# Projections of a fused attention and feed-forward block in another order: values, gates, latent query and key, then key and query

## The chip, the cores and the metric

The kernel runs on one core of a Trainium2 chip. The metric is the device time of one execution in microseconds (us). The kernel before was timed three times: 748.38, 748.62 and 749.38 us, median 748.62. One execution was also profiled. The core's engines run side by side, each through its own list of instructions in order: TensorE (PE for its matmuls and PEld for its weight loads), VectorE (DVE), ScalarE (ACT), GpSimd (POOL) and SyncE (SP, which issues most DMAs here). They wait for one another by semaphores.

## The reference, cut to what matters

The input x is 32 batches of 256 rows by 128 columns, all float32. Each batch goes through one adaptive-layernorm block:

```
h = layernorm(x) * (1 + ca) + sa                # scale and shift per batch, from a small matmul
Q, K, V = h @ wq, h @ wk, h @ wv                # 16 heads of 8
local = softmax(window-masked Q K^T / sqrt(8)) @ V    # window of 32, blocks of 32 against 64
GQ = h @ wgq                                    # 8 heads of 8, latent query
GK, GV = mean4(h @ wgk), mean4(h @ wgv)         # 64 latents: means over 4 rows
rem = softmax(causal GQ GK^T / sqrt(8)) @ GV @ r_out_w
out = (sigmoid(Q . gate_local) * local + sigmoid(Q . gate_remote) * rem) @ w_out
x = x + ga * out
x = x + gb * ffn(layernorm(x) * (1 + cb) + sb)  # per-batch mixed weights, 512 wide, gelu
```

## The kernel before

Everything stays on chip. The batches run through a software pipeline of 36 steps, `for it in range(4)`, a hardware loop over it = 4 to 31 (28 passes of the same instructions), and four more steps. In step `it` the kernel works on several batches at once: layernorm of batch it, projections and scores of batch it - 1, softmax output and gating of batch it - 2, output projection of batch it - 3, second layernorm and the gate of the feed-forward of batch it - 4. After the pipeline comes the feed-forward part, eight batches at a time, which the change does not touch.

There is no scheduler. Each engine has a function `step(it)` whose order is written by hand, and the order of the work is that of the five lists and the semaphores between them. PSUM is eight banks, SB0 to SB3 (scores and their transposes) and WB0 to WB3 (everything else); `bank_free` makes TensorE wait until the last reader of a bank is through.

What the steps around the change do, with the lines of the kernel before:

- TensorE, `projections(it)` (lines 831 to 856), the first thing in its step: key and query (wk, wq) into WB0, after VectorE has read the latent scores there (semaphore `ls_sub`); latent query and key (wgq, wgk) into WB1; values (wv) into WB3; two gates (gate_w) into WB2, after ScalarE has read the last batch's gates from there (`tg_ready`). Then `latent_T` (line 899): transposes of the latent probabilities into WB0 once ScalarE has copied the query out of it (`qt_ready`) and into WB1; `probs_T` (line 888): transposes of the probabilities Pr into SB0 to SB3; later `latent_values`, the transpose of xn_d (line 994), `values` with its row sums on PT_sum (lines 927 and 931), and at the end of the step `latent_scores` and `scores` of batch it - 1 (lines 970, 871 to 882).
- ScalarE, `step` (line 405): copies K_ch and QT (key and query) out of WB0, then exponentials Pr 1, GQT and GKT (latent query and key) out of WB1, Pr 2, V_rows (values) out of WB3, Pr 3, then the copies PL and PT of the transposed probabilities, xn_d and h2T (second layernorm), hT, and the exponentials PlA, PlB, the gates' tanh (tg) and Pr 0. The exponentials of batch it - 2 wait for VectorE (`s_sub`), one each.
- GpSimd, `step` (line 331): KM, four copies of the key each masked to some of the heads, from K_ch (line 336); then the small operations on the layernorm statistics, ve_a and rstd_a of batch it and ve_d, neg_d, rstd_d, shift_d of batch it - 4; then PT_sum in two halves (line 358), GKBD, the residual addition, attT.
- VectorE, `step` (line 595): statistics of both layernorms, xn_a, the latent and local normalisations (rlden; rden, line 634, and a_loc, which frees bank SB2 for the next scores), gating, then latent maxima, lowered latent scores (PlA, PlB), and maxima and lowered scores Pr 0 to Pr 3.
- SyncE: stores V_rows when copied and loads it again spread out (VBD).

Of the kernel before, what the change touches and what calls it, by code (L numbers as in the profile page):

```python
# [14 lines left out]
D = 128  # L15
# [9 lines left out]
def adaln_block(nc, ins, out):  # L25
# [17 lines left out]
    with ExitStack() as ctx:  # L43
# [143 lines left out]
        def at_least(eng, s, value):  # L187

            if not isinstance(value, int) or value > 0:
                eng.wait_ge(s, value)  # L190
# [203 lines left out]
        @block.scalar  # L394
        def _(act):
            act.wait_ge(mod_loaded, N_MOD)
            nc.scalar.activation(silu_a[:], c_rows[:], ACT.Exp, scale=-1.0).then_inc(silu_exp, 1)
            act.wait_ge(siluT_done, 1)
            nc.scalar.copy(siluT[:], WB[1][:, 0:B]).then_inc(siluT_ready, 1)

            def probs(b, k):
                act.wait_ge(s_sub, 4 * b + (k + 1))
                nc.scalar.activation(Pr[:, k, :], Pr[:, k, :], ACT.Exp).then_inc(p_ready, 1)  # L403

            def step(it):
                if has(it, 1):

                    b = it - 1
                    act.wait_ge(qk_done, b + 1)
                    at_least(act, km_ready, b)  # L410
                    nc.scalar.copy(K_ch[:], WB[0][:, S:2 * S]).then_inc(k_ready, 1)  # L411
                    nc.scalar.copy(QT[:], WB[0][:, 0:S]).then_inc(qt_ready, 1)
                if has(it, 2):
                    probs(it - 2, 1)
                if has(it, 1):
                    act.wait_ge(gqk_done, b + 1)
                    nc.scalar.activation(GQT[0:NL], WB[1][0:NL, 0:S], ACT.Copy, scale=SCALE / POOL).then_inc(gq_ready, 1)
                    nc.scalar.copy(GKT[:], WB[1][0:NL, S:S + NL]).then_inc(gq_ready, 1)
                if has(it, 2):
                    probs(it - 2, 2)  # L420
                if has(it, 1):

                    b = it - 1
                    act.wait_ge(v_done, b + 1)
                    at_least(act, vbd_loaded, N_VBD * b)
                    nc.scalar.copy(V_rows[:].rearrange("p t n -> p (t n)"), WB[3][:, 0:T * D]).then_inc(vrows_ready, 1)
                if has(it, 2):
                    probs(it - 2, 3)
                if has(it, 2):
                    b = it - 2  # L430
                    if isinstance(it, int) and it == 2:
                        act.wait_ge(ga_stored, 16)

                    act.wait_ge(lpt_done, 2 * b + 1)
                    nc.scalar.copy(PL[:, :, 0:S].rearrange("p g (t s) -> p t g s", t=T),  # L435
                                   WB[0][:].rearrange("p (t g s) -> p t g s", t=T, g=LG)).then_inc(lpt_copied, 1)
                    act.wait_ge(lpt_done, 2 * b + 2)
                    nc.scalar.copy(PL[:, :, S:S + P],
                                   WB[1][:, 0:2 * P].rearrange("p (g s) -> p g s", g=LG)).then_inc(lpt_copied, 1)
                    for q in range(4):  # L440

                        act.wait_ge(pt_done, 4 * b + (q + 1))
                        nc.scalar.copy(PT[:, q * 2 * S:(q + 1) * 2 * S], SB[q][:]).then_inc(pt_copied, 1)  # L443
                if has(it, 4):
                    b = it - 4
                    act.wait_ge(shift_ready, b + 1)
                    at_least(act, x2T_done, b)
                    for t in range(T):
                        nc.scalar.activation(xn_d[:, t, :], x_all[:, bass.ds(b * S + t * D, D)], ACT.Identity,  # L449
                                             scale=rstd_d[:, t:t + 1], bias=shift_d[:, t:t + 1]).then_inc(xn_d_s, 1)  # L450
                    act.wait_ge(x2T_done, b + 1)
                    nc.scalar.activation(h2T[:, bass.ds(b * S, S)], SB[0][:, 0:S], ACT.Identity,
                                         scale=cb1T[:, bass.ds(b, 1)], bias=sbT[:, bass.ds(b, 1)]).then_inc(h2T_ready, 1)
                    act.wait_ge(hid_done, b + 1)

                    nc.scalar.activation(SB[1][:, 0:S], SB[1][:, 0:S], ACT.Relu, bias=gate_b1[:],  # L456
                                         accum_out=hsum[:, bass.ds(b, 1)]).then_inc(hid_summed, 1)
                if has(it, 0):

                    act.wait_ge(xT_done, it + 1)  # L460
                    at_least(act, hp_ready, it)
                    if isinstance(it, int) and it == 0:
                        act.wait_ge(mod_ready, 4)
                    nc.scalar.activation(hT[:], SB[0][:, 0:S], ACT.Identity, scale=ca1T[:, bass.ds(it, 1)],
                                         bias=saT[:, bass.ds(it, 1)]).then_inc(hT_ready, 1)
                if has(it, 1):
                    b = it - 1
                    for t, pl in ((0, PlA), (1, PlB)):
                        act.wait_ge(ls_sub, 2 * b + (t + 1))
                        nc.scalar.activation(pl[:], pl[:], ACT.Exp).then_inc(pl_ready, 1)  # L470

                    act.wait_ge(gates_done, b + 1)
                    at_least(act, ag_ready, b)
                    at_least(act, remg_ready, b)
                    nc.scalar.activation(tg[:].rearrange("p k s -> p (k s)"), WB[2][:], ACT.Tanh, scale=0.5
                                         ).then_inc(tg_ready, 1)
                    probs(b, 0)

            def after(it):
                if it == 0:  # L480
                    act.wait_ge(wqT_done, 1)
                    nc.scalar.copy(wqT, SB[1][:, 0:D]).then_inc(wqT_ready, 1)
                    act.wait_ge(gate_w_done, 1)
                    for k in range(2):
                        nc.scalar.copy(gate_w[:, k, :].rearrange("p (h d) -> p h d", d=HD),
                                       bc(SB[2][:, k * H:(k + 1) * H], [P, H, HD], 2)).then_inc(gate_w_ready, 1)
                if it == 1:

                    act.wait_ge(wT_done, 1)
                    nc.scalar.copy(W1T[:], WB[3][:]).then_inc(wT_ready, 1)  # L490
                    act.wait_ge(wT_done, 2)
                    nc.scalar.copy(W2T[:].rearrange("p c h -> p (c h)"), WB[3][:]).then_inc(wT_ready, 1)
                    act.wait_ge(wT_done, 3)
                    nc.scalar.copy(gate_w1T[:], WB[3][:, 0:P]).then_inc(wT_ready, 1)
                    nc.scalar.copy(gate_w2T[:], WB[3][:, P:P + E]).then_inc(wT_ready, 1)

            pipeline(act, step, after)

            with act.Fori(0, NG) as g:
                for j in range(GB):  # L500

                    act.wait_ge(ffn1_done, g * GB + (j + 1))
                    if j >= 2:
                        act.wait_ge(ffn2_done, g * GB + (j - 1))
                    for c in range(FC):
                        nc.scalar.activation(u[j % 2][:, c, :], WB[2 * (j % 2) + c // 2][:, (c % 2) * S:(c % 2 + 1) * S],  # L506
                                             ACT.Gelu_apprx_tanh, bias=mb1T[:, c, bass.ds(g * GB + j, 1)]
                                             ).then_inc(gelu_done, 1)
# [266 lines left out]
        def _(pe):  # L775
# [55 lines left out]
            def projections(it):  # L831
                b = it - 1
                pe.wait_ge(hT_ready, b + 1)
                bank_free(pe, it, (2, ls_sub, 2, 2))
                mm(WB[0][:, S:2 * S], wk[:], hT[:], start=True, stop=True)  # L835
                mm(WB[0][:, 0:S], wq[:], hT[:], start=True, stop=True).then_inc(qk_done, 1)
                pe.wait_ge(hp_ready, b + 1)
                bank_free(pe, it, (2, ls_sub, 2, 1))
                mm(WB[1][0:NL, 0:S], wgq[:], hT[:], start=True, stop=True)
                mm(WB[1][0:NL, S:S + NL], wgk[:], hpT[:], start=True, stop=True).then_inc(gqk_done, 1)  # L840
                bank_free(pe, it, (3, remg_ready, 1, 1), (2, vrows_ready, 1, 1))
                if isinstance(it, int) and it == 1:
                    pe.wait_ge(attn_w_ready, 1)
# [10 lines left out]
                for k in range(2):  # L854
                    last = mm(WB[2][:, k * S:(k + 1) * S], gate_w[:, k, :], hT[:], start=True, stop=True)
                last.then_inc(gates_done, 1)

            def scores(it):

# [278 lines left out]
```

## Time and profile before

| | before |
|---|---|
| median of three runs | 748.62 us |
| the profiled execution | 748.97 us, its span 747.2 us |
| mean granted TensorE clock over the span | 0.979 of full speed |
| busy share: TensorE matmul, weight load | 86%, 68% |
| busy share: VectorE, ScalarE, GpSimd | 72%, 52%, 39% |
| chain that ended last, by engine | PE 42%, DVE 26%, ACT 15%, no visible wait 14% |
| pipeline steps | from about 8 us to 563 us; one pass of the loop 16.34 us |
| feed-forward part | about 563 us to the end |

The shares are averages over two parts with different limits. In the feed-forward part TensorE is nearly always busy; in the pipeline no engine is, and what sets its pace has to be read from one pass. Times are counted from the start of the span.

### The profile page before, as it was taken

To read this page: it belongs to the slowest core of one execution; us is meant where nothing else is said; L and a number is where in the kernel's file an instruction comes from. 1 tells how busy PE (TensorE), PEld (TensorE's weight loads), DVE (VectorE), ACT (ScalarE), POOL (GpSimd) and SP (SyncE) were. 2 spreads that over 40 slices of the span, in tenths; PEclk is the share of its full clock that TensorE was granted. 3 is DMA by queue.
4 is the path that set the end of the run, shared out by engine and by line. 5 is a ranking of instruction groups with operands and counts; after the bars stand their busy time and mean duration, and the time that the engine had idled before them with its cause. 6 is when DMAs were issued, how large, how long until landed. Compare 5 with 4: busy or idle time off the path is not lost.

```text
span 747.2 us, 24120 instructions
## 1 busy us (share of the span) xinstructions
PE 645.6 (86%) x8822; PEld 506.4 (68%) x8822; DVE 538.1 (72%) x1241; ACT 384.9 (52%) x910; POOL 294.9 (39%) x415
## 2 busy tenths in 40 slices
PE   5588888788888878888887888888779999999998
PEld 3366666566666656666665666666558999898996
DVE  5568788888878888887888888788755546273552
ACT  2256655666665566666555666655543223423233
POOL 2256555455555545555554555555530000000000
PEclk9699999999999999999999999999978999999999
DMA  3757111000101100010110001010140010100101
GB/s 99 174 78 96 32 24 32 21 21 21 28 22 24 31 21 21 21 28 21 24 32 21 21 21 28 21 24 18 29 44 0 10 35 15 32 24 21 34 9 49
DMA packets 65797, 24.84 MB, mean 33 GB/s; under 512 B 38440, under 2 KB 64360, under 8 KB 65648
## 3 DMA queue, kind: packets, MB, share of 16 engines
q1 hardware_dynamic: 64320, 18.25, 10.2%
q0 software_dynamic: 1456, 6.31, 5.6%
q8 instruction: 14, 0.23, 0.1%
q14 instruction: 7, 0.06, 0.0%
HBM read 16.13 MB, written 8.40 MB: 33 GB/s over the span
## 4 chain that ended last, share of the span: by engine, by line
PE 42%; DVE 26%; ACT 15%; issue 14%; POOL 1%; ACTq 1%; DVEq 1%; DMA 0%; SPq 0%; POOLq 0%
DVE mx L561 10%; PE SB L820 7%; PE WB L808 7%; DVE rden L634 5%; ACT PT L443 5%; PE SB L927 5%; PE WB L795 4%; PE SB L795 4%; ACT xn_d L449 4%; DVE Pr L568 3%; ACT Pr L403 3%; PE SB L882 2%; PE SB L931 2%; ACT PL L435 2%; PE WB L970 2%
## 5 line engine op out<-in xcount | busy, mean ns | idle before, releaser
L336 POOL TENSOR_TENSOR KM<-K_ch,bd_scale 128x1024 f32<-128x1024 f32 x32 | 60.6, 1893 | 125.2 <-ACT K_ch L411 125.2
L634 DVE RECIPROCAL rden<-SB 128x256 f32<-128x256 f32 x32 | 56.2, 1758 | 54.5 <-PE SB L931 54.5
L506 ACT ACTIVATE Pr<-WB,mb1T 128x256 f32<-128x256 f32 x128 | 49.8, 477 | 75.7 <-PE WB L808 75.6
L561 DVE TENSOR_REDUCE mx<-SB 128x8 f32<-128x512 f32 x128 | 87.2, 681 | 1.5 <-PE SB L882 1.5
L403 ACT ACTIVATE Pr<-Pr 128x512 f32<-128x512 f32 x128 | 80.8, 631 | 10.8 <-DVE Pr L568 7.2
L568 DVE TENSOR_TENSOR Pr<-SB,mx 128x512 f32<-128x512 f32 x128 | 84.6, 681 | 0.0
L358 POOL TENSOR_TENSOR PT_sum<-PT 128x512 f32<-128x512 f32 x64 | 80.3, 1275 | 3.8 <-ACT PT L443 3.8
L443 ACT COPY PT<-SB 128x512 f32<-128x512 f32 x128 | 66.1, 622 | 0.0
L896 PE MATMUL SB<-ident,Pr 128*128 128x128 f32 x512 | 63.0, 276 | 0.9 <-ACT Pr L403 0.9
L820 PE MATMUL SB<-Pr,GA 128*128 128x256 f32 x256 | 61.2, 381 | 0.0
L835 PE MATMUL WB<-hT,wk 128*128 128x256 f32 x64 | 23.3, 448 | 43.2 <-DVE PlB L582 43.2
L808 PE MATMUL WB<-h2T,mW 128*128 (+1 forms) x256 | 60.2, 380 | 0.0
L896 PEld LDWEIGHTS SB<-ident,Pr 128*128 128x128 f32 x512 | 57.8, 143 | 1.8 <-ACT Pr L403 1.8
L377 POOL TENSOR_TENSOR attT<-a_gated,rem_g 128x256 f32<-128x256 f32 x32 | 23.2, 725 | 88.8 <-DVE a_gated L647 85.7
L470 ACT ACTIVATE PlA<-PlA 128x256 f32<-128x256 f32 x32 | 13.3, 416 | 79.5 <-DVE PlA L582 79.5
L808 PEld LDWEIGHTS WB<-h2T,mW 128*128 128x128 f32 x256 | 48.2, 190 | 6.4
L820 PEld LDWEIGHTS SB<-Pr,GA 128*128 128x128 f32 x256 | 46.1, 190 | 6.2 <-DVE GA L675 1.2
L835 PEld LDWEIGHTS WB<-hT,wk 128*128 128x128 f32 x64 | 10.0, 196 | 57.7 <-DVE PlB L582 53.7
L882 PE MATMUL SB<-KM,QT 32*32 32x256 f32 x2048 | 48.4, 387 | 0.0
L970 PE MATMUL WB<-GKBD,GQT 128*128 128x512 f32 (+1 forms) x128 | 47.9, 498 | 0.0
L456 ACT ACTIVATE SB<-SB,gate_b 128x256 f32<-128x256 f32 x32 | 14.3, 448 | 63.8 <-PE SB L1011 63.8
L615 DVE RECIPROCAL rlden<-WB 128x128 f32<-128x128 f32 x32 | 30.7, 958 | 19.7 <-PE WB L946 19.7
(195 smaller groups left out, 1518.5 us busy)
## 6 DMA issues: line engine op xcount, KB each, us to landing
x_all<-in_L_attn_x SPq DMA_DIRECT2D x32, 128.0 KB, 2.1
v_rows<-V_rows SPq DMA_DIRECT2D x32, 128.0 KB, 1.8
VBD<-v_rows SPq DMA_DIRECT2D x128, 32.0 KB, 1.8
TW<-in_L_ffn_TW POOLq DMA_DIRECT2D x16, 256.0 KB, 9.5
GA<-ga_rows POOLq DMA_DIRECT2D x1, 2048.0 KB, 10.5
out_x<-attT SPq DMA_DIRECT2D x16, 128.0 KB, 1.8
out_x<-y_ga SPq DMA_DIRECT2D x16, 128.0 KB, 1.8
PT<-in_L_ffn_W SPq DMA_DIRECT2D x2, 256.0 KB
```

The source lines that it names most:

```text
L336: nc.gpsimd.tensor_tensor(KM[:, :, W:KW], bc(K_ch[:], [P, 4, S], 1), bc(bd_scale[:], [P, 4, S], 2), ALU.mult).then_inc(km_ready, 1)
L358: nc.gpsimd.tensor_tensor(PT_sum[:, pair, :], both[:, pair, 0, :], both[:, pair, 1, :], ALU.add).then_inc(pts_ready, 1)
L403: nc.scalar.activation(Pr[:, k, :], Pr[:, k, :], ACT.Exp).then_inc(p_ready, 1)
L443: nc.scalar.copy(PT[:, q * 2 * S:(q + 1) * 2 * S], SB[q][:]).then_inc(pt_copied, 1)
L561: nc.vector.tensor_reduce(mx[:, k, :], SB[k][:].rearrange("p (h j) -> p h j", h=8), AX.X, ALU.max).then_inc(mx_ready, 1)
L568: nc.vector.tensor_tensor(Pr[:, k, :].rearrange("p (w h c) -> p h w c", w=2, h=8), SB[k][:].rearrange("p (h w c) -> p h w c", w=2, h=8), b ...
L634: nc.vector.reciprocal(rden[:], SB[2][:, S:2 * S]).then_inc(rden_ready, 1)
L808: last = mm(WB[2 * (j % 2) + c // 2][:, (c % 2) * S:(c % 2 + 1) * S], mW1[:, j, c * P:(c + 1) * P], h2T[:, bass.ds((g * GB + j) * S, S)], ...
L820: last = mm(SB[j % 2][:, 0:S], mW2[:, c, j, :], u[j % 2][:, c, :], start=(c == 0), stop=(c == FC - 1))
L882: last = mm(SB[g][W * q:W * q + W, 4 * HALF * t:4 * HALF * (t + 1)].rearrange("p (h j) -> p h j", h=4), QT[rows, W * blk:W * blk + W], KM[ ...
L896: last = nc.tensor.transpose(SB[q][:, k * P:(k + 1) * P], Pr[:, q, o:o + P], ident[:])
L970: mm(WB[1 - t][:, 0:8 * m].rearrange("p (h j) -> p h j", h=8), GQT[:, t * P:(t + 1) * P], GKBD[:, :, 0:m], start=True, stop=True).then_inc ...
```

## The change

The order of the four projections on TensorE becomes values, gates, latent query and key, key and query; ScalarE's copy of the values moves to where key and query were copied, and the other way round. All instructions, banks, sizes and semaphores stay; every wait moves with its instruction.

```diff
@@ ScalarE, step
                 if has(it, 1):
 
                     b = it - 1
-                    act.wait_ge(qk_done, b + 1)
-                    at_least(act, km_ready, b)
-                    nc.scalar.copy(K_ch[:], WB[0][:, S:2 * S]).then_inc(k_ready, 1)
-                    nc.scalar.copy(QT[:], WB[0][:, 0:S]).then_inc(qt_ready, 1)
+                    act.wait_ge(v_done, b + 1)
+                    at_least(act, vbd_loaded, N_VBD * b)
+                    nc.scalar.copy(V_rows[:].rearrange("p t n -> p (t n)"), WB[3][:, 0:T * D]).then_inc(vrows_ready, 1)
                 if has(it, 2):
                     probs(it - 2, 1)
...
-                    act.wait_ge(v_done, b + 1)
-                    at_least(act, vbd_loaded, N_VBD * b)
-                    nc.scalar.copy(V_rows[:].rearrange("p t n -> p (t n)"), WB[3][:, 0:T * D]).then_inc(vrows_ready, 1)
+                    act.wait_ge(qk_done, b + 1)
+                    at_least(act, km_ready, b)
+                    nc.scalar.copy(K_ch[:], WB[0][:, S:2 * S]).then_inc(k_ready, 1)
+                    nc.scalar.copy(QT[:], WB[0][:, 0:S]).then_inc(qt_ready, 1)
                 if has(it, 2):
                     probs(it - 2, 3)
@@ TensorE, projections
                 pe.wait_ge(hT_ready, b + 1)
-                bank_free(pe, it, (2, ls_sub, 2, 2))
-                mm(WB[0][:, S:2 * S], wk[:], hT[:], start=True, stop=True)
-                mm(WB[0][:, 0:S], wq[:], hT[:], start=True, stop=True).then_inc(qk_done, 1)
-                pe.wait_ge(hp_ready, b + 1)
-                bank_free(pe, it, (2, ls_sub, 2, 1))
-                mm(WB[1][0:NL, 0:S], wgq[:], hT[:], start=True, stop=True)
-                mm(WB[1][0:NL, S:S + NL], wgk[:], hpT[:], start=True, stop=True).then_inc(gqk_done, 1)
                 bank_free(pe, it, (3, remg_ready, 1, 1), (2, vrows_ready, 1, 1))
...
                 last.then_inc(gates_done, 1)
+                pe.wait_ge(hp_ready, b + 1)
+                bank_free(pe, it, (2, ls_sub, 2, 1))
+                mm(WB[1][0:NL, 0:S], wgq[:], hT[:], start=True, stop=True)
+                mm(WB[1][0:NL, S:S + NL], wgk[:], hpT[:], start=True, stop=True).then_inc(gqk_done, 1)
+                bank_free(pe, it, (2, ls_sub, 2, 2))
+                mm(WB[0][:, S:2 * S], wk[:], hT[:], start=True, stop=True)
+                mm(WB[0][:, 0:S], wq[:], hT[:], start=True, stop=True).then_inc(qk_done, 1)
```

TensorE at the head of the hardware loop before; "x2" is two instructions of one form, and the lines that are not matmuls load or compute the value of a wait.

```order
L190 ISA
L835 MATMUL WB<-hT,wk 128x256
L836 MATMUL WB<-hT,wq 128x256
L190 REGISTER_ALU
L839 MATMUL WB<-hT,wgq 64x256
L840 MATMUL WB<-hpT,wgk 64x64
L847 MATMUL WB<-wv,hT 128x128 x2
L190 REGISTER_ALU
L855 MATMUL WB<-hT,gate_w 128x256 x2
L901 REGISTER_ALU
L904 MATMUL WB<-ident,PlA 128x128 x2
```

The same place in the changed kernel.

```order
L190 REGISTER_ALU
L840 MATMUL WB<-wv,hT 128x128 x2
L190 REGISTER_ALU
L848 MATMUL WB<-hT,gate_w 128x256 x2
L190 ISA
L852 MATMUL WB<-hT,wgq 64x256
L853 MATMUL WB<-hpT,wgk 64x64
L190 REGISTER_ALU
L855 MATMUL WB<-hT,wk 128x256
L856 MATMUL WB<-hT,wq 128x256
L904 MATMUL WB<-ident,PlA 128x128 x2
```

Key and query have moved from first to last, right ahead of the latent transposes (L904), which wait for the copy of the query.

ScalarE from the head of the loop before to its copy PL; Pr rows are the exponentials 1, 2 and 3.

```order
L411 COPY K_ch<-WB 128x256
L412 COPY QT<-WB 128x256
L402 ISA
L403 ACTIVATE Pr<-Pr 128x512
L417 ACTIVATE GQT<-WB 64x256
L418 COPY GKT<-WB 64x64
L402 REGISTER_ALU
L403 ACTIVATE Pr<-Pr 128x512
L190 REGISTER_ALU
L426 COPY V_rows<-WB 128x256
L402 REGISTER_ALU
L403 ACTIVATE Pr<-Pr 128x512
```

The same place in the changed kernel.

```order
L411 COPY V_rows<-WB 128x256
L402 ISA
L403 ACTIVATE Pr<-Pr 128x512
L416 ACTIVATE GQT<-WB 64x256
L417 COPY GKT<-WB 64x64
L402 REGISTER_ALU
L403 ACTIVATE Pr<-Pr 128x512
L425 COPY K_ch<-WB 128x256
L426 COPY QT<-WB 128x256
L402 REGISTER_ALU
L403 ACTIVATE Pr<-Pr 128x512
```

K_ch and QT now stand behind the exponential Pr 2; V_rows stands ahead of Pr 1. VectorE's, GpSimd's and SyncE's own lists are the same as before.

## Rows read from the trace of the kernel before

**Rows 1.** Timeline, VectorE, one loop pass: start, us, engine, line, operation, count, [idle before <-releaser]

```profile
306.49 1.76 DVE L634 RECIPROCAL rden<-SB 128x256 f32<-128x256 f32 x1 [1.75 <-PE SB L931]
...
322.83 1.76 DVE L634 RECIPROCAL rden<-SB 128x256 f32<-128x256 f32 x1 [1.75 <-PE SB L931]
```

**Rows 2.** Timeline, the same pass, from VectorE's last lowered scores to the row sums

```profile
315.12 1.28 DVE L568 TENSOR_TENSOR Pr<-SB,mx 128x512 f32<-128x512 f32 x2
...
315.83 0.63 ACT L403 ACTIVATE Pr<-Pr 128x512 f32<-128x512 f32 x1 [0.20 <-DVE Pr L568]
...
316.37 0.35 ACT L426 COPY V_rows<-WB 128x256 f32<-128x256 f32 x1
316.62 0.63 ACT L403 ACTIVATE Pr<-Pr 128x512 f32<-128x512 f32 x1
...
317.15 0.57 ACT L435 COPY PL<-WB 128x512 f32<-128x512 f32 x1
...
317.88 2.06 ACT L443 COPY PT<-SB 128x512 f32<-128x512 f32 x4
...
319.79 0.93 ACT L449 ACTIVATE xn_d<-x_all,shift_d,rstd_d 128x128 f32 x2
...
320.77 0.44 PE L994 MATMUL SB<-ident,xn_d 128*128 128x128 f32 x2 [0.89 <-ACT xn_d L449]
...
322.15 0.62 PE L931 MATMUL SB<-PT_sum,ones_bd 128*32 128x256 f32 x8
```

**Rows 3.** Timeline, the same pass, key and query copies and GpSimd's work behind them

```profile
313.98 0.35 ACT L411 COPY K_ch<-WB 128x256 f32<-128x256 f32 x1
...
314.23 0.38 ACT L412 COPY QT<-WB 128x256 f32<-128x256 f32 x1
314.41 1.89 POOL L336 TENSOR_TENSOR KM<-K_ch,bd_scale 128x1024 f32<-128x1024 f32 x1 [3.80 <-ACT K_ch L411]
...
317.15 0.20 POOL L327 TENSOR_TENSOR ve_a<-mv_a,eps_row 128x2 f32<-128x2 f32 x1 [0.85 <-DVE mv_a L551]
...
319.16 0.20 POOL L350 TENSOR_TENSOR shift_d<-neg_d,rstd_d 128x2 f32<-128x2 f32 x1
...
319.31 2.51 POOL L358 TENSOR_TENSOR PT_sum<-PT 128x512 f32<-128x512 f32 x2
```

**Rows 4.** Timeline, the same pass, TensorE's projections and what follows, and ScalarE's tanh

```profile
312.26 0.70 PE L835 MATMUL WB<-hT,wk 128*128 128x256 f32 x2 [1.44 <-DVE PlB L582]
...
312.78 0.58 ACT L475 ACTIVATE tg<-WB 128x512 f32<-128x512 f32 x1
...
313.81 0.28 PE L840 MATMUL WB<-hpT,wgk 128*64 128x64 f32 x2
...
314.56 1.03 PE L855 MATMUL WB<-hT,gate_w 128*128 128x256 f32 x4
...
315.43 0.38 PE L904 MATMUL WB<-ident,PlA 128*128 128x128 f32 x2
...
316.08 1.91 PE L896 MATMUL SB<-ident,Pr 128*128 128x128 f32 x16
```

**Rows 5.** Timeline, steps 2 and 3, GpSimd behind KM and ahead of rden

```profile
37.43 1.89 POOL L336 TENSOR_TENSOR KM<-K_ch,bd_scale 128x1024 f32<-128x1024 f32 x1 [9.68 <-ACT K_ch L411]
...
39.29 0.18 POOL L327 TENSOR_TENSOR ve_a<-mv_a,eps_row 128x2 f32<-128x2 f32 x1
...
58.01 2.52 POOL L358 TENSOR_TENSOR PT_sum<-PT 128x512 f32<-128x512 f32 x2 [0.91 <-ACT PT L443]
...
61.29 1.76 DVE L634 RECIPROCAL rden<-SB 128x256 f32<-128x256 f32 x1 [1.34 <-PE SB L931]
```

**Rows 6.** Timeline, step 1, one VectorE setup instruction

```profile
16.06 1.88 DVE L728 TENSOR_SCALAR win_bf<-cur 128x32 bf16<-128x32 f32 x1
```

**Rows 7.** Stretches: us, busy PE PEld DVE ACT POOL (count), PEclk, DMA share, GB/s

```profile
306.49:322.83 16.34, 13.95 (x241) 10.32 (x242) 13.61 (x33) 10.16 (x24) 8.79 (x13) 1.00 0.11 24
540.00:544.00 4.00, 1.53 (x10) 1.06 (x10) 4.00 (x8) 2.43 (x5) 1.59 (x3) 0.94 0.93 126
```

## The prediction

> **What bounds the kernel now.** I read the page first, for its two parts: the feed-forward part is TensorE alone and is not touched, so all is decided in the pipeline. Then the chain of waits for the pipeline, which repeats from one normalisation (rden, line 634) to the next, and last the timeline of one pass, to see for each engine what it waits for and what stands ready. From rden to rden a pass takes 322.83 - 306.49 = 16.34 us [rows 1], and in it TensorE is busy for 13.95, VectorE for 13.61, ScalarE for 10.16, GpSimd for 8.79 [rows 7]. No engine is full; the pace is a loop of dependences:
>
> - VectorE runs from rden through a_loc, gating, maxima and lowered scores. Pr 2 and Pr 3 are two instructions in 1.28, so Pr 2 ends at 315.12 + 0.68 (the other 0.60 is the step to the next) = 315.80, 9.31 after this pass's rden at 306.49 [rows 1, 2].
> - ScalarE takes over at 315.83 and is never idle to the end of xn_d: exponential Pr 2, V_rows, Pr 3, PL, its second part, four PT, xn_d [rows 2].
> - TensorE waits 0.89 for xn_d, then goes through the transpose and the local values to the row sums at 322.15, and rden follows at 322.83 after VectorE has idled for 1.75 [rows 1, 2].
>
> GpSimd has a branch beside this. Its KM starts after K_ch (313.98 to 314.41, a step of 0.43) and ends at 316.30. It then idles for 0.85 until VectorE's statistics come, starts ve_a at 317.15, and goes on without a wait to PT_sum, 319.31 to 321.82 [rows 3]. The row sums that need PT_sum start at 322.15, so this branch has only about 0.3 us to spare.
>
> **TensorE's part of the change.** Before, TensorE pauses for 1.44 ahead of wk, since VectorE still reads the latent scores in WB0 [rows 4]. Values need bank WB3, long free, so they move into this pause. The gates come second now and need WB2, which ScalarE's tanh still reads until 312.78 + 0.58 = 313.36. So the pause is not removed, it moves behind the values and lasts until 313.41. From there: gates take what they took to the next matmul, 315.43 - 314.56 = 0.87, to 314.28. Key, query and latent query take 313.81 - 312.26 = 1.55, and the latent key at most its 0.28, so all projections are done by about 316.15 to 316.25 [rows 4]. Before they had cleared TensorE at 315.43. The latent key is ready by about 315.15, near the time at which GQT was copied anyway, with Pr 2 still due at 315.83 behind it.
>
> **ScalarE's part.** V_rows moves ahead of Pr 1, into a place where ScalarE waits for VectorE; I cost it at nothing, its cover being the wait for Pr 1, and it saves its 0.25 (316.37 to 316.62) behind Pr 2 [rows 2]. In its place stand K_ch and QT. K_ch starts at 316.37, when V_rows did, because Pr 2 in front of it cannot start before 315.83, and the query should be there just before, with 0.1 to 0.2 in hand. QT starts 0.25 later [rows 3] and ends at 317.00. Pr 3 comes about 0.3 later than before.
>
> Two things hang on this.
>
> - *QT.* The latent transposes wait for it. They started at 315.43 and now start about 317.2, 1.8 later, and the transposes of Pr with them [rows 4]. The latent ones stood ready about 1.1 before ScalarE read them (their end, near 316.05, against PL at 317.15), and the last group of Pr's (end 317.99, copied from about 319.4) 1.4 before [rows 2, 4]. So ScalarE's copies slip by 1.8 - 1.1 = 0.7, not by 1.8. On this branch alone a pass would grow by 0.7 to 0.8.
> - *K_ch.* KM is first in GpSimd's step, so all behind it waits. KM starts at 316.37 + 0.43 = 316.80 in place of 314.41. In step 2 ve_a was ready and followed KM's start by 39.29 - 37.43 = 1.86 [rows 5]; here it then starts at 318.66 in place of 317.15, 1.51 later. GpSimd ran on without a wait before, so the rest moves by the same: shift_d to 320.67, PT_sum to 320.82, its end to 323.33 [rows 3]. In step 3 the row sums had to wait for PT_sum, and rden came 61.29 - (58.01 + 2.52) = 0.76 after its end [rows 5]; here that is 324.09. Before it was 322.83: 1.26 more.
>
> xn_d needs shift_d: 320.87, then 0.98 to its transpose (319.79 to 320.77) makes 321.85, and the row sums could start 1.38 later, at 323.23 [rows 2], just ahead of PT_sum's 323.38. So GpSimd's branch decides, by little. The three branches join in rden, and from there VectorE's 9.31 to Pr 2 is the same as before. The loop is then 9.31 + 0.03 + 0.54 (Pr 2 to K_ch) + 0.43 + 1.86 + 2.16 (ve_a to PT_sum) + 2.51 + 0.76 = 17.60 us a pass.
>
> **What is hidden.** The values' store and reload start about 2.4 earlier and have a whole pass to land; the reload waits for the last pass's values as before. VectorE waits longer for rstd_a, by 1.5, and has 1.75 of idle ahead of rden to take that from [rows 1]. KM itself is needed only by the next scores, some 6 us later.
>
> **The steps outside the loop.** The loop has 28 passes: 28 x 1.26 = 35.3 us. Steps 1, 2, 3 and 32 also project. Step 3 has no second layernorm and step 32 no first one, so GpSimd has less behind KM; there I expect what ScalarE's branch gives, 0.8 to 0.9 each. In steps 1 and 2 TensorE is slow and K_ch comes later still, which delays ve_a; as bounds take 0 (setup hides it) and 1.9 (a whole KM, 1.89 [rows 3]), and I take 1.2 each. Together 4.1, between 1 and 6.
>
> Sum: 748.97 + 35.3 + 4.1 = 788.4 against the profiled execution, which lies 0.35 above the median of the runs; so 788.0.
>
> **VectorE beside KM.** KM used to run beside VectorE's maxima and lowered scores, which read PSUM. Now it runs from 316.80 to 318.66 beside the statistics, which read SBUF. One row shows what can happen there: in step 1 a VectorE tensor_scalar on only 32 elements a partition took 1.88 and ended as KM did [rows 6]. The Trainium skill, "Advanced Engine Details and Errata", VectorE Performance Modes, says that the second Vector SBUF port is shared with GpSimd and that two-port Vector instructions and GpSimd's block each other; the row agrees. By that rule the time hangs on whether the statistics are two-port instructions; no trace here has them beside KM.
>
> If they are held, the aggregation of the first statistics can only start when KM is through. It and the next instruction's start took 0.3 (two instructions of about 0.15, each of them small, ahead of ve_a), so ve_a would come 0.3 to 0.4 behind KM.
>
> **Rivals.**
>
> - *ScalarE's branch decides* (GpSimd catches up in some way, as if KM's later start cost it less): 0.8 a pass, 28 x 0.8 + 4 = 26, so 775 us. For it: it is the same kind of wait; against it: GpSimd had 0.3 to spare and is moved by 1.5. Chance 0.12.
> - *VectorE's statistics are held by KM*: 0.35 more a pass, 10 us, so 798. For it [rows 6]; against it: the statistics write six numbers from 128, and look unlike a copy that is sped up by a second port. Chance 0.08.
> - *TensorE's clock falls.* It was granted in full (1.00, 2.4 GHz) through the pass with TensorE busy for 13.95 of 16.34; near the pipeline's end it fell to 0.50 after a stretch in which TensorE was busy for 1.53 of 4.00 [rows 7]. The new order makes 13.95 of 17.60, and the thinnest 4 us of the pass begin at 312.26 - 1.44 = 310.82, where the scores end: they had 314.82 - 312.26 = 2.56 of work before and have about 0.7 of values and 314.82 - 313.41 = 1.41 of gates and latent query now, 2.1 [rows 4]. That lies between the stretch that kept the clock and the one of 1.53. At half the clock the projections from the gates on and the transposes would lose about 2 us a pass; in one pass of three that is 19 us, so 807; in all, 844. Chance 0.12.
> - *Not slower:* TensorE's own list sets the pace, its 1.44 pause ahead of the projections is the price of the old order, and work moved into it is won. The values are worth at most what latent key and values took, 314.56 - 313.81 = 0.75 [rows 4], so 28 x 0.75 = 21 us, 728. It decides only if the wait for tanh ended before the values do. Against it: tanh ends 1.1 later than the old wait did, and TensorE waits 0.89 for ScalarE later in the pass [rows 2]. Chance 0.02.
>
> My forecast has 0.65, and 0.01 is left for the unforeseen. Its own range, from the 0.1 to 0.2 that the query has in hand (28 x 0.2 = 6) and the steps outside the loop, is 783 to 795. For 8 in 10 the range goes up to the held statistics and to the edge of the clock's case and down towards ScalarE's branch: 778 to 807. About 0.2% (1.5 us) is what can be told from no change; only the last rival and the unforeseen are not slower: faster 0.02, same 0.01, slower 0.97.
>
> **What would show it.** In the changed profile: a pass of about 17.6 from rden to rden; KM waiting for K_ch, ve_a right behind KM with no wait for mv_a; row sums waiting for PT_sum on GpSimd; xn_a waiting some 1.5 longer for rstd_a; the gates waiting for tg, L904 for QT. I am wrong if the row sums wait for xn_d's transpose alone, if the granted clock in the loop is below 1.00, if a statistics instruction on VectorE is far over 0.3 us, or if K_ch waits for the query by more than 0.2.

## The result, and the profile after

The changed kernel takes 805.85 us, median of four runs (803.70 to 808.74), against 748.90 before. The ratio is 1.077, 95% interval 1.074 to 1.079: slower by 7.7%. The profiled execution took 806.54, so 57.57 more than the profiled one of before.

The page of the changed kernel: span, busy time of each engine, and the granted TensorE clock in 40 slices.

```profile
span 804.8 us, 24148 instructions
...
PE 674.7 (84%) x8822; PEld 521.0 (65%) x8822; DVE 539.9 (67%) x1241; ACT 395.8 (49%) x910; POOL 294.2 (37%) x415
...
PEclk9899899898998999999998999999996999999999
```

The busy times of VectorE and GpSimd have moved by less than 2 us. ScalarE shows 11 us more and TensorE 29 us more, and the granted clock, 9 in nearly all slices before, now has slices of 8 in the pipeline.

From rden to rden the passes of the hardware loop (28, steps 4 to 31) fall into three kinds. Each length is the distance of two starts of line 634 on VectorE's timeline.

| kernel | passes | length, us | granted clock |
|---|---|---|---|
| before | 28 | 16.32 to 16.38 | 1.00 |
| changed | 19 | 17.53 to 17.60 | 1.00 |
| changed | 4 | 18.94 to 19.09 | 0.91 |
| changed | 5 | 19.64 to 19.66 | 0.83 |

One pass of the first kind on the changed kernel's timeline, in the order of [rows 1 to 4]: start, us, engine, line, operation, [idle before <-releaser].

```profile
322.69 1.76 DVE L634 RECIPROCAL rden<-SB 128x256 f32<-128x256 f32 x1 [1.38 <-PE SB L931]
...
329.61 1.13 PE L848 MATMUL WB<-hT,gate_w 128*128 128x256 f32 x4 [1.94 <-ACT tg L475]
...
331.31 1.27 DVE L568 TENSOR_TENSOR Pr<-SB,mx 128x512 f32<-128x512 f32 x2
...
332.02 0.63 ACT L403 ACTIVATE Pr<-Pr 128x512 f32<-128x512 f32 x1
...
332.56 0.35 ACT L425 COPY K_ch<-WB 128x256 f32<-128x256 f32 x1
332.81 0.38 ACT L426 COPY QT<-WB 128x256 f32<-128x256 f32 x1
332.99 1.89 POOL L336 TENSOR_TENSOR KM<-K_ch,bd_scale 128x1024 f32<-128x1024 f32 x1 [6.19 <-ACT K_ch L425]
...
333.33 0.41 PE L904 MATMUL WB<-ident,PlA 128*128 128x128 f32 x2 [0.84 <-ACT QT L426]
...
334.00 0.58 ACT L435 COPY PL<-WB 128x512 f32<-128x512 f32 x1 [0.28 <-PE WB L906]
...
334.84 0.19 POOL L327 TENSOR_TENSOR ve_a<-mv_a,eps_row 128x2 f32<-128x2 f32 x1
...
336.99 2.52 POOL L358 TENSOR_TENSOR PT_sum<-PT 128x512 f32<-128x512 f32 x2
337.24 0.88 ACT L449 ACTIVATE xn_d<-x_all,shift_d,rstd_d 128x128 f32 x2 [0.43 <-POOL shift_d L350]
...
338.17 0.44 PE L994 MATMUL SB<-ident,xn_d 128*128 128x128 f32 x2 [0.49 <-ACT xn_d L449]
...
339.57 0.63 PE L931 MATMUL SB<-PT_sum,ones_bd 128*32 128x256 f32 x8
...
340.27 1.76 DVE L634 RECIPROCAL rden<-SB 128x256 f32<-128x256 f32 x1 [1.39 <-PE SB L931]
```

The pass is 340.27 - 322.69 = 17.58 us; forecast were 17.60. Each step stands where it was put: the gates (L848) wait 1.94 for tanh; K_ch and QT follow the exponential Pr 2; the latent transposes (L904) wait 0.84 for QT; KM runs from 332.99 and ve_a starts 1.85 behind its start, without a wait; PT_sum ends at 339.51 and the row sums start at 339.57. xn_d waits 0.43, for shift_d on GpSimd, and its transpose comes 1.40 ahead of the row sums, against 322.15 - 320.77 = 1.38 before [rows 2]. So xn_d's branch alone would have let them start at 339.55: the two branches out of GpSimd, over PT_sum and over shift_d, end within 0.02 of each other, and both stand behind KM. The forecast had 0.15 between them.

Two passes that follow each other; columns as in [rows 7].

```profile
121.62:139.20 17.58, 14.31 (x241) 10.36 (x242) 13.59 (x33) 10.50 (x24) 8.76 (x13) 1.00 0.10 22
139.20:158.86 19.66, 16.93 (x241) 12.49 (x242) 13.60 (x34) 10.59 (x24) 9.32 (x14) 0.83 0.09 20
```

The second has the same instructions, but for one at its border, and 2.62 us more of TensorE at a lower clock. Some of its rows, on the timeline:

```profile
148.25 1.22 PE L855 MATMUL WB<-hT,wk 128*128 128x256 f32 x2
...
149.26 1.06 PE L856 MATMUL WB<-hT,wq 128*128 128x256 f32 x2
...
150.36 0.37 ACT L425 COPY K_ch<-WB 128x256 f32<-128x256 f32 x1 [1.00 <-PE WB L856]
...
151.15 0.66 PE L904 MATMUL WB<-ident,PlA 128*128 128x128 f32 x2 [0.83 <-ACT QT L426]
...
152.46 2.79 PE L896 MATMUL SB<-ident,Pr 128*128 128x128 f32 x16
...
155.07 2.52 POOL L358 TENSOR_TENSOR PT_sum<-PT 128x512 f32<-128x512 f32 x2 [0.21 <-ACT PT L443]
```

Key and query take 0.99 to 1.01 each from start to start (at the full clock 0.53, 331.36 to 331.89). The query is late now: K_ch waits 1.00 for it and starts 150.36 - 139.20 = 11.16 after rden, where it was 332.56 - 322.69 = 9.87, and the steps behind it are late with it. The 16 transposes of Pr take 2.79 where they took 1.91 [rows 4], and PT_sum has to wait 0.21 for copies of them. The clock had gone to 0.50 (1.2 GHz) about 147.4, after TensorE had rested for 1.90 between values and gates and then worked for 1.3. What TensorE does ahead of a fall does not tell the passes apart: the gates start 6.92 after rden behind a wait of 1.94 in the pass from 357.85, which fell, and 6.91 after rden behind a wait of 1.94 in the next, from 376.94, which kept 1.00.

### The profile page after: what moved, and what is told of

The parts are those of the page before. It is cut to its first block, busy times and chain, and to the rows that moved or that the text cites. A ratio compares the mean times of both kernels' runs of the same rounds, so it can differ in the third digit from the quotient of the medians.

```text
span 804.8 us, 24148 instructions
## 1 busy us (share of the span) xinstructions
PE 674.7 (84%) x8822; PEld 521.0 (65%) x8822; DVE 539.9 (67%) x1241; ACT 395.8 (49%) x910; POOL 294.2 (37%) x415
## 4 chain that ended last, share of the span: by engine, by line
PE 41%; issue 33%; POOL 11%; DVE 9%; ACT 4%; POOLq 1%; DMA 0%; ACTq 0%; DVEq 0%; SPq 0%
PE SB L820 7%; PE WB L808 7%; POOL KM L336 6%; PE SB L927 4%; PE WB L795 4%; PE SB L795 4%; DVE rden L634 3%; PE SB L896 2%; PE SB L931 2%; ACT xn_d L449 2%; PE SB L994 2%; POOL x_all L370 1%; PE WB L848 1%; DVE mx L561 1%; PE WB L855 1%
## 5 line engine op out<-in xcount | busy, mean ns | idle before, releaser
L848 PE MATMUL WB<-hT,gate_w 128*128 128x256 f32 x128 | 37.9, 421 | 58.3 <-ACT tg L475 58.0
L555 DVE TENSOR_SCALAR xn_a<-x_all,mv_a,rstd_a 128x128 f32 (+1 forms) x64 | 24.3, 419 | 80.6 <-POOL rstd_a L329 80.6
L896 PE MATMUL SB<-ident,Pr 128*128 128x128 f32 x512 | 66.9, 287 | 1.4 <-ACT Pr L403 1.4
L848 PEld LDWEIGHTS WB<-hT,gate_w 128*128 128x128 f32 x128 | 22.7, 198 | 66.3 <-ACT tg L475 63.7
L896 PEld LDWEIGHTS SB<-ident,Pr 128*128 128x128 f32 x512 | 62.5, 151 | 2.3 <-ACT Pr L403 2.3
```

The source lines that it names most:

```text
L896: last = nc.tensor.transpose(SB[q][:, k * P:(k + 1) * P], Pr[:, q, o:o + P], ident[:])
```

## The experiments

**TensorE kept busy while it waits for the gates' bank (filler).** Three matmuls that nobody reads:

```diff
                 for t in range(T):
                     last = mm(WB[3][:, t * D:(t + 1) * D], hT[:, t * P:(t + 1) * P], wv[:], start=True, stop=True)
+                if not isinstance(it, int):
+                    for k in range(3):
+                        last = mm(WB[3][:, S:2 * S], wv[:], hT[:], start=True, stop=True)
                 last.then_inc(v_done, 1)
```

> The changed kernel with three extra matmuls (values weights on hT, into columns 256 to 511 of bank WB3, which nobody reads) behind the values in each pass of the hardware loop, so that they fill most of TensorE's wait for the gates' bank. In the changed kernel 19 of the passes from rden to rden take 17.58 us at a full granted clock, five take 19.65 and four about 19.0 at a lower one. Theory A (the thin stretch of TensorE around that wait makes the clock fall, and a fallen clock costs the 16 us over 17.58 a pass): every pass 17.58, granted clock 1.00 in the loop, about 790 us. Rival (the falls have another cause, or the extra work costs as much as it gives): passes of 19 to 20 us remain, 803 us or more.

Measured: 794.58 us (791.73 to 795.22), ratio 1.060 (1.057 to 1.063). All 28 loop passes take 17.53 to 17.60 at clock 1.00. One of them:

```profile
314.94:332.53 17.59, 15.61 (x247) 11.35 (x248) 13.60 (x33) 10.50 (x24) 8.76 (x13) 1.00 0.10 22
```

15.61 us of TensorE in place of 14.31, the same 17.59, and no fall. So more work on TensorE made the kernel 11 us faster: the falls in the loop need the wait ahead of the gates, and they cost what the long passes take over 17.58, 5 x 2.07 + 4 x 1.43 = 16 us in the changed kernel's profiled execution. Of the 4.6 us over my 790, 3.5 are outside the loop: steps 3 and 32, which have no filler, took 18.92 and 18.60 at 0.91, where the changed kernel has 17.40 and 17.00, and setup was 0.4 longer.

**KM behind PT_sum and GKBD (km_late).** The changed kernel with KM's wait and instruction moved from the head of GpSimd's step to behind GKBD:

```diff
-                    pool.wait_ge(k_ready, b + 1)
-                    nc.gpsimd.tensor_tensor(KM[:, :, W:KW], ...).then_inc(km_ready, 1)
                 ...
                     nc.gpsimd.tensor_tensor(GKBD[0:NL], ...).then_inc(gkbd_ready, 1)
+                    pool.wait_ge(k_ready, b + 1)
+                    nc.gpsimd.tensor_tensor(KM[:, :, W:KW], ...).then_inc(km_ready, 1)
```

> The changed kernel with one move: GpSimd's KM stands behind PT_sum and GKBD in its step and no longer ahead of the layernorm statistics. Theory A (late K_ch costs the pass through KM at the head of GpSimd's list): shift_d and PT_sum are on time again, xn_d no longer waits for shift_d (0.43 us a pass in the changed kernel), and ScalarE's branch (latent transposes behind QT) decides: 17.15 us a pass where the clock is full, against 17.58 changed and 16.35 before; with the falls of the clock as they were about 794 us. Rival (ScalarE's branch decides already and GpSimd only rides along): 17.58 stays, 806 us. Rival (the whole loss is GpSimd's): 16.4 a pass, 770 us.

Measured: 773.16 us (771.54 to 773.52), ratio 1.032 (1.030 to 1.034). 27 of the 28 loop passes take 17.00 to 17.05, the first 18.59 at 0.91. One of the 27:

```profile
303.48:320.50 17.02, 14.29 (x241) 10.35 (x242) 13.61 (x33) 10.39 (x24) 8.81 (x13) 1.00 0.10 23
```

On its timeline (VectorE's last two lowered scores, then ScalarE's copies, L901 the latent transposes, ve_a, PL, xn_d and its transpose):

```profile
329.14 1.28 DVE L565 TENSOR_TENSOR Pr<-SB,mx 128x512 f32<-128x512 f32 x2
...
330.39 0.35 ACT L422 COPY K_ch<-WB 128x256 f32<-128x256 f32 x1
...
331.16 0.41 PE L901 MATMUL WB<-ident,PlA 128*128 128x128 f32 x2 [0.85 <-ACT QT L423]
331.18 0.20 POOL L327 TENSOR_TENSOR ve_a<-mv_a,eps_row 128x2 f32<-128x2 f32 x1 [6.54 <-DVE mv_a L548]
...
331.83 0.59 ACT L432 COPY PL<-WB 128x512 f32<-128x512 f32 x1 [0.28 <-PE WB L903]
...
334.49 0.92 ACT L446 ACTIVATE xn_d<-x_all,shift_d,rstd_d 128x128 f32 x2
...
335.46 0.44 PE L991 MATMUL SB<-ident,xn_d 128*128 128x128 f32 x2
```

ve_a is on time again, and xn_d has no wait ahead of it. 0.56 us of the 1.23 were GpSimd's. The other 0.67 are ScalarE's branch: from the end of Pr 2's lowering (329.14 + 0.68 = 329.82) to PL it is 2.01, where it was 317.15 - 315.80 = 1.35 before [rows 2]. 0.28 of that is a wait of PL for the latent transposes behind QT, and the rest is two copies in the place of one. Neither rival holds: 17.58 did not stay, and 16.4 did not come. The time lies near the second rival's 770, but by another way than the rival's.

The 794 of theory A missed by 21 us, since it kept the falls of the clock: after the first, no loop pass fell, though the gates wait as long (1.80 to 1.97) as in the changed kernel. The next run looks into that.

**The same, with two small copies more on ScalarE (km_late_plus).**

```diff
                     act.wait_ge(qk_done, b + 1)
                     at_least(act, km_ready, b)
+                    if not isinstance(it, int):
+                        for k in range(2):
+                            nc.scalar.copy(spare[:, k * P:(k + 1) * P], ident[:])
                     nc.scalar.copy(K_ch[:], WB[0][:, S:2 * S]).then_inc(k_ready, 1)
```

> km_late (17.03 us a pass, no fall of the clock in the loop) with two small extra copies on ScalarE ahead of K_ch in each pass of the hardware loop, some 0.35 us. Theory A (the thin stretch of TensorE around the gates is the same in km_late as in the changed kernel, and which passes fall depends also on how the passes come to lie, not on where KM stands): 17.35 to 17.45 us at full clock and some passes of 19 us at a lower clock, four or more of the 28, so 786 to 800 us. Rival (km_late had no falls because TensorE no longer waits for xn_d late in the pass): all passes 17.4 and clock 1.00, 782 us.

Measured: 804.57 us (802.20 to 811.16), ratio 1.076 (1.071 to 1.082). 17 loop passes take 17.39 to 17.44 at clock 1.00, as forecast, and 11 are longer, between 18.97 and 21.45. Two of them:

```profile
300.19:317.63 17.44, 14.25 (x241) 10.36 (x242) 13.61 (x34) 10.78 (x26) 8.85 (x13) 1.00 0.10 23
317.63:339.07 21.44, 18.30 (x241) 13.62 (x242) 13.58 (x34) 11.20 (x26) 9.77 (x13) 0.76 0.08 18
```

The time lies above the 786 to 800 of the expectation: with 0.4 us more a pass, all of it on ScalarE and with TensorE's own work the same, the falls came back, and in 11 of 28 passes. The rival fails, since xn_d's transpose has no wait in either run. But this run does not hold all else equal: TensorE's wait ahead of the latent transposes (L905) is 1.24 here where it was 0.85 in km_late, so the longer pass and the longer second wait are not told apart. The profiled execution was also the slowest of the four, with a mean granted clock of 0.935 where the others have 0.943 to 0.953, so how much time is spent at the low clock differs from one execution to the next.

The passes of one kernel say more: km_late has the wait ahead of the gates in every pass and fell in one, here 17 passes kept the clock and 11 did not, and in the changed kernel 19 and 9. So whether a pass falls depends on more than the content of the pass; on what is open. The three executions of km_late agree (771.54 to 773.52), so its 773 is no single lucky execution, but two small copies took it away, and I could not have forecast it.

**ScalarE's order alone (act_only).** The kernel before with only the first two hunks of the change, those of ScalarE's step.

> The kernel before with ScalarE's copies in the new order and TensorE's projections in the old one. Theory A (ScalarE's order alone makes K_ch and QT late, since both stand behind the exponential Pr 2): the same 17.58 us a pass at full clock, with TensorE waiting 1.44 ahead of key and 1.8 ahead of the latent transposes; the two waits enclose 3.2 us of unbroken work, so falls of the clock are rarer: 789 to 806 us. Rival (TensorE's new order, with the gates' wait for tanh, carries a part): under 17.3 a pass and under 780 us.

Measured: 793.39 us (792.75 to 793.83), ratio 1.060 (1.057 to 1.062). 17.73 to 17.77 a pass, all at clock 1.00:

```profile
296.75:314.50 17.75, 14.10 (x241) 10.28 (x242) 13.60 (x33) 10.28 (x24) 8.76 (x13) 1.00 0.10 22
```

```profile
305.10 0.37 ACT L411 COPY V_rows<-WB 128x256 f32<-128x256 f32 x1 [0.77 <-PE WB L847]
...
305.37 1.28 DVE L568 TENSOR_TENSOR Pr<-SB,mx 128x512 f32<-128x512 f32 x2
...
306.25 0.64 ACT L403 ACTIVATE Pr<-Pr 128x512 f32<-128x512 f32 x1
...
307.55 0.41 PE L904 MATMUL WB<-ident,PlA 128*128 128x128 f32 x2 [1.70 <-ACT QT L426]
```

K_ch follows Pr 2 (at 306.79) and the latent transposes wait 1.70 for QT, as in the changed kernel, and this without TensorE's new order. The pass is 0.17 longer than in the changed kernel since V_rows now waits 0.77 for values that TensorE computes third; that pushes Pr 1 and with it Pr 2, which starts 0.20 after the end of its lowering (305.37 + 0.68 = 306.05 against 306.25) where it was 0.03 before. I had missed this wait. ScalarE's order alone makes all of the loss at full clock, and 0.17 more. In the loop the clock never falls here. TensorE is busy for less of the pass than in the changed kernel (14.10 against 14.31), so the falls do not follow the busy share of a pass; the longest wait is 1.70 in place of 1.94, and the 1.44 ahead of the key and the 1.70 ahead of the transposes have 3.3 us of work between them (302.52 to 305.85). That this is the reason is argued; no run shows it.

**TensorE's order alone (pe_only).** The kernel before with only the last two hunks.

> The kernel before with TensorE's projections in the new order and ScalarE's copies in the old one. Key and query are ready only about 0.5 us after Pr 2 was lowered, and K_ch, QT, three exponentials, GQT, GKT and V_rows stand behind them on ScalarE: Pr 3 comes 2.0 us later than before. Theory A: 18.35 us a pass at full clock and more falls of the clock, 811 to 840 us, so slower than both. Rival (TensorE's order costs only the 0.8 us by which its projections end later): 17.15 a pass, 772 us.

Measured: 841.99 us (840.88 to 842.97), ratio 1.124 (1.122 to 1.127), slowest of all. A pass at full clock takes 18.28 to 18.36, and 19 of the 28 are longer at a lower clock:

```profile
301.29:319.65 18.36, 14.53 (x241) 10.34 (x242) 13.61 (x33) 10.04 (x24) 8.84 (x13) 1.00 0.09 21
319.65:339.54 19.89, 16.09 (x241) 11.16 (x242) 13.59 (x34) 10.04 (x24) 8.79 (x13) 0.91 0.09 20
```

```profile
309.93 1.28 DVE L568 TENSOR_TENSOR Pr<-SB,mx 128x512 f32<-128x512 f32 x2
...
311.22 0.37 ACT L411 COPY K_ch<-WB 128x256 f32<-128x256 f32 x1 [2.33 <-PE WB L856]
...
312.64 0.64 ACT L403 ACTIVATE Pr<-Pr 128x512 f32<-128x512 f32 x1
...
313.42 0.64 ACT L403 ACTIVATE Pr<-Pr 128x512 f32<-128x512 f32 x1
```

K_ch is first on ScalarE and waits 2.33 for the query, with everything behind it: Pr 3 starts 313.42 - (309.93 + 0.68) = 2.81 after Pr 2's lowering, before 316.62 - 315.80 = 0.82 [rows 2]. That is the forecast 2.0 a pass; the time lies 2 us above the 840 at which the expectation ended. So TensorE's order needs ScalarE's, and together they are cheaper than this half.

**Only the values moved into TensorE's wait (values_first).** The kernel before, with the values' four lines ahead of key and query in `projections`.

> The kernel before with one move: the values' matmuls stand first in TensorE's projections and the rest of both orders is as before. They fall into TensorE's wait for bank WB0 (1.44 us a pass). Theory A (that wait is off the path, since ScalarE's exponential Pr 2 stands behind VectorE's lowered scores): 16.35 us a pass, clock 1.00, 748.5 us within 1. Rival (TensorE's list sets the pace, as the prediction's last rival has it): up to 0.75 a pass less, 728 us.

Measured: 749.49 us (748.39 to 750.63), ratio 1.001 (1.000 to 1.002): no change. A pass:

```profile
306.96:323.32 16.36, 14.53 (x241) 10.40 (x242) 13.61 (x33) 10.17 (x24) 8.81 (x13) 1.00 0.10 24
```

TensorE's 1.44 ahead of the key is worth nothing by itself: the rival "Not slower" is wrong as a mechanism, too. The clock stays full.

**V_rows copied in ScalarE's idle time (rows_early).** values_first, and:

```diff
+            def value_rows(b):
+                act.wait_ge(v_done, b + 1)
+                at_least(act, vbd_loaded, N_VBD * b)
+                nc.scalar.copy(V_rows[:].rearrange("p t n -> p (t n)"), WB[3][:, 0:T * D]).then_inc(vrows_ready, 1)
...
-                if has(it, 1):
-
-                    b = it - 1
-                    act.wait_ge(v_done, b + 1)
-                    at_least(act, vbd_loaded, N_VBD * b)
-                    nc.scalar.copy(V_rows[:].rearrange("p t n -> p (t n)"), WB[3][:, 0:T * D]).then_inc(vrows_ready, 1)
+                if isinstance(it, int) and it in (1, 2):
+                    value_rows(it - 1)
...
                     for t, pl in ((0, PlA), (1, PlB)):
+                        if t == 1 and (not isinstance(it, int) or 2 <= it < B):
+                            value_rows(it)
```

> As values_first, and ScalarE copies V_rows one step earlier, between the exponentials PlA and PlB, where it idles for 0.78 us, and no longer between Pr 2 and Pr 3 (batches 0 and 1 at the head of steps 1 and 2). Theory A (ScalarE's stretch from Pr 2 to xn_d is on the path): Pr 3 starts when VectorE has lowered it, 0.18 us earlier, all behind it too: 16.17 us a pass, 28 x 0.18 = 5 us, 743.5 us. Rival (the copy delays PlB, tanh and Pr 0, or TensorE's transposes of Pr are late next): 16.35 a pass or more, 748.5 us or more.

Measured: 743.66 us (742.23 to 744.08), ratio 0.993 (0.990 to 0.995): 0.7% faster than the kernel before. A pass and some of its rows:

```profile
304.03:320.19 16.16, 14.39 (x241) 10.41 (x242) 13.58 (x33) 10.35 (x24) 8.83 (x13) 1.00 0.10 24
```

```profile
308.30 0.71 PE L843 MATMUL WB<-wv,hT 128*128 128x128 f32 x4
...
309.12 0.37 ACT L404 COPY V_rows<-WB 128x256 f32<-128x256 f32 x1
...
309.76 0.63 ACT L473 ACTIVATE PlB<-PlB 128x512 f32<-128x512 f32 x1 [0.27 <-DVE PlB L585]
...
312.64 1.27 DVE L571 TENSOR_TENSOR Pr<-SB,mx 128x512 f32<-128x512 f32 x2
...
313.35 1.23 ACT L408 ACTIVATE Pr<-Pr 128x512 f32<-128x512 f32 x2 [0.20 <-DVE Pr L571]
```

V_rows at 309.12 lies in the wait for PlB, which starts no later than it could; Pr 2 and Pr 3 run back to back (1.23 for two), and the pass is 16.16, 0.19 less. Here the early values are of use: they let ScalarE's copy leave the stretch that sets the pace.

## Why the prediction came out as it did

The direction and the place were right; the likeliest case was not the one that came. The forecast of 788 had the clock at 1.00 in the loop, and the 783 to 795 of that case was missed. The wide range, 778 to 807, held by 1.2 us, and one of the four executions (808.74) lies above it; that it held owes something to luck. The rival "TensorE's clock falls" came true, with a chance of 0.12, in the form that it was priced: one pass of three, 807 us.

- *A pass at full clock:* 17.60 forecast, 17.58 measured. Over the 28 passes 1.23 x 28 = 34.4 us, forecast 35.3. The changed kernel's rows show GpSimd's order as the end of it, though xn_d's transpose came almost as late as PT_sum, and km_late shows the sizes of the parts: GpSimd over ScalarE 0.56 (forecast 1.26 - 0.7 to 0.8, so about 0.5), ScalarE's branch 0.67 (forecast 0.7 to 0.8).
- *The clock:* 9 of 28 passes at 0.91 or 0.83, together 16.1 us, forecast for the likeliest case 0. filler shows that they need the wait ahead of the gates. The step that failed is the weighing: in the thinnest 4 us of the pass I had 2.1 of work, between 1.53 in a stretch that lost the clock and 2.56 in one that kept it [rows 4, 7], nearly in the middle, and gave the fall a chance of 0.12. Nothing in those three numbers supports so low a one.
- *Price of a fall:* 19 us for one pass in three (2 each) forecast, 16.1 for nine measured, 2.07 or 1.43 each.
- *The steps outside the loop:* 4.1 forecast, between 1 and 6; 7.0 measured (setup to the first rden 3.9, step 3 1.6, step 32 0.7, step 33 -0.8, from the last rden to the end 1.5). Setup was estimated from bounds only. In step 1 key and query now stand behind values, gates and latent query and key, whose matmuls take longer there than in the loop (values 1.20, gates 2.08, against 0.71 and 1.13), so K_ch starts at 20.48 where it was 15.47, and ve_a behind KM at 22.85 where it was 20.61: 2.2 in that step alone, over the bound of 1.9. The last two terms go with the clock, which I had not priced there: step 33 had 0.80 before and has 1.00 now, and behind the last rden the clock stands at 0.50 for about 13.6 us where it was about 10.2.
- *VectorE beside KM:* the statistics are not held. The first ones (st_a) end as KM starts at 332.99, the second ones (st_d) run beside it. Both in the pass above, and the row of the second ones over all 64:

```profile
332.51 0.47 DVE L546 BATCH_NORM_STATS2 st_a<-x_all 128x6 f32 x2
...
333.24 0.49 DVE L546 BATCH_NORM_STATS2 st_d<-x_all 128x6 f32 x2
```

```profile
L546 DVE BATCH_NORM_STATS2 st_d<-x_all x64: 269/277/297, 77.3 to 618.7; 128x6 f32 x56, 128x6 f32<-128x128 f32 x8
```

  With KM beside them the second ones take 277 ns in the median, as without it (280 before). The instruction that KM had held up in setup for 1.88 [rows 6] is free where KM runs later:

```profile
16.23 0.17 DVE L728 TENSOR_SCALAR win_bf<-cur 128x32 bf16<-128x32 f32 x1
```

  The Trainium skill's rule ("Advanced Engine Details and Errata", VectorE Performance Modes), that two-port Vector instructions and GpSimd's block each other, agrees with both rows: 1.88 beside KM and 0.17 without it for the tensor_scalar, and nothing for the statistics, which would be one-port instructions by that rule; no row shows their mode.
- *ScalarE's branch decides:* wrong by itself; it is 0.56 shorter than GpSimd's. *Not slower:* the values in the wait are worth nothing (values_first).

34.4 + 16.1 + 7.0 = 57.5, of 57.57 measured.

## What to carry to other kernels

Follow the copy that moves, not the matmul: the loss at full clock came from the copies of key and query, placed behind an instruction that waits for VectorE, on an engine with 48% idle time. The first instruction of GpSimd's list hung on the key's copy (0.56 a pass); the latent transposes behind the query's copy, and two copies in the place of one in ScalarE's own list, made the other 0.67. When a change leaves an engine's work as it was and moves its waits together, ask what the thinnest stretch of TensorE becomes, and if it lies between stretches that kept and lost the clock, give the fall a large chance. Work moved into a wait pays only if it lets something leave the path, as V_rows in rows_early.

## What the runs showed of the hardware that I had not expected

- 1.3 us of useless matmuls a pass made the program 11 us faster (805.85 to 794.58), by keeping TensorE's clock at 2.4 GHz.
- Falls of the clock are not a property of one pass's content: with the same instructions and a wait of 1.83 to 1.95 ahead of the gates in each, 9 of the changed kernel's 28 loop passes fell and 19 did not. With such a wait one of km_late's 28 passes fell (17.02 long), and 11 of km_late_plus's (17.4 long, with a second wait of 1.24 in place of 0.85). What decides is left open.
- GpSimd's instruction KM (1.9 us) held up a VectorE tensor_scalar on 32 elements a partition for 1.88 us (0.17 without KM beside it) and left the statistics beside it at 277 ns (280 before).
